# Attention output: probabilities normalised before they are turned, values as the stationary operand, heads summed in PSUM

## What is computed

```python
x = L0_attn_Z
xn = _layernorm(x); s = mamba(xn); g = _silu(moe0(xn))
x = x + s * g
xn = _layernorm(x, axis=-1)
s = _L1_attn_ref(xn, gamma, w_qkv, w_out)     # below
g = _silu(_L1_ffn_ref(xn, wg, we))            # top-2 of 128 experts
return x + s * g

# _L1_attn_ref
xn = x / jnp.maximum(l2, 1e-12) * scale_norm * gamma
q, k, v = per head of xn @ w_qkv.T            # q * 128 ** -0.5
sim = jnp.einsum('bihd,bjhd->bhij', q, k)
sim = jnp.where(causal_mask, neg, sim)
attn = jax.nn.softmax(sim, axis=-1)
out = jnp.einsum('bhij,bjhd->bihd', attn, v)
return jnp.einsum('bnf,cf->bnc', out.reshape(b, n, 1024), w_out)
```

## Time and profile before

| | us |
|---|---|
| median of 3 runs (1464.28 to 1469.84) | 1465.71 |
| span of the profiled execution | 1465.0 |
| PE busy over the span | 1277.5 (87%) |
| DVE busy over the span | 1227.2 (84%) |
| ACT busy over the span | 856.9 (58%) |
| attention stage, share of PE in 1275 to 1400 us | 125.00 of 125.00 |
| one iteration in that stretch | 7.20 |
| one iteration with expert products (about 1156 to 1271 us) | 8.19 |

### The profile page before, as it was taken

The page is one execution under the profiler, slowest core; times in us unless marked ns, Lnnn a source line. Parts: engine busy times, 40 slices in busy tenths (PEclk is TensorE's granted clock), DMA queues, the critical chain, the costliest instruction groups (busy, mean ns, idle before and its releaser), DMA issues. The chain is left out here.

```text
span 1465.0 us, 21638 instructions
## 1 busy us (share of the span) xinstructions
PE 1277.5 (87%) x7304; PEld 888.3 (61%) x7304; DVE 1227.2 (84%) x2515; ACT 856.9 (58%) x2077; POOL 661.9 (45%) x612
## 2 busy tenths in 40 slices
PE   6977888897887976899897895599999999999997
PEld 5533444453433444788887774467676777777776
DVE  6678999998999899999997778869988555568877
ACT  5357757665798885556654658554464444444462
POOL 0018555605489855664751775339600322147300
PEclk9997999999999877999999898699999999999999
DMA  6003545545244422454552520300020233113201
GB/s 230 1 21 87 147 128 147 141 122 153 82 126 126 123 87 68 126 155 135 146 146 72 190 53 13 119 7 1 2 59 1 60 89 107 41 38 49 25 16 43
DMA packets 75747, 127.50 MB, mean 87 GB/s; under 512 B 11486, under 2 KB 38334, under 8 KB 75030
## 3 DMA queue, kind: packets, MB, share of 16 engines
q1 hardware_dynamic: 56182, 75.24, 17.0%
q0 software_dynamic: 19456, 50.88, 13.2%
HBM read 85.71 MB, written 40.37 MB: 86 GB/s over the span
## 5 line engine op out<-in xcount | busy, mean ns | idle before, releaser
L672 DVE TENSOR_TENSOR_SCAN sc_st<-sc_dA,sc_st 128x1024 f32<-128x1024 f32 x128 | 287.3, 2284 | 0.0
L2164 DVE COPY at_pT<-at_p_t 128x512 f32<-128x512 f32 (+1 forms) x192 | 109.0, 598 | 107.8 <-PE at_p_t L2046 107.4
L1270 POOL DMA_INDIRECT g_state<-xn_scratch,moe_tab x96 | 119.6, 1246 | 174.3 <-POOLq L99 102.4
L2059 PEld LDWEIGHTS at_p_o<-at_V,at_pT 128*128 128x128 f32 x1280 | 154.4, 194 | 31.1 <-issue 30.8
L444 ACT ACTIVATE sc_dA<-sc_dt,g_state 128x511 f32<-128x511 f32 x256 | 168.9, 710 | 7.2 <-DVE sc_st L672 5.3
L650 DVE TENSOR_TENSOR sc_st<-sc_st,sc_p_bc 128x1024 f32<-128x1024 f32 x128 | 154.9, 1211 | 13.4 <-PE sc_p_bc L501 13.2
L640 DVE TENSOR_TENSOR sc_st<-sc_u,sc_p_bc 128x1024 f32<-128x1024 f32 x128 | 154.3, 1206 | 6.6 <-PE sc_p_y L532 6.3
L1310 POOL DMA_INDIRECT g_state<-r_scratch,moe_tab x96 | 121.5, 1266 | 83.6 <-PE e_bank L1409 56.7
L2059 PE MATMUL at_p_o<-at_V,at_pT 128*128 128x128 f32 x1280 | 155.0, 277 | 3.6 <-DVE g_state L2153 3.6
L2026 PE MATMUL at_p_s<-att_xaT,at_qT 128*128 128x512 f32 (+3 forms) x512 | 150.7, 437 | 0.0
L501 PE MATMUL sc_p_bc<-sc_bc,mamba_sel 96*128 96x512 bf16 x256 | 104.9, 411 | 50.5 <-DVE sc_st L640 48.6
(11 more groups left out here) (304 smaller groups left out, 2615.0 us busy)
## 6 DMA issues: line engine op xcount, KB each, us to landing
y_scratch<-g_state SPq DMA_DIRECT2D x24, 768.0 KB, 5.2
g_state<-W SPq DMA_DIRECT2D x48, 256.0 KB, 5.5
r_scratch<-g_state SPq DMA_DIRECT2D x16, 512.0 KB, 3.6
y_scratch<-g_state SPq DMA_DIRECT2D x24, 192.0 KB, 2.8
xn_scratch<-g_state SPq DMA_DIRECT2D x16, 256.0 KB, 4.9
g_state<-x SPq DMA_DIRECT2D x4, 512.0 KB, 7.5
g_state<-xn_scratch SPq DMA_DIRECT2D x8, 256.0 KB, 5.2
g_state<-x SPq DMA_DIRECT2D x1, 2048.0 KB, 12.7
```

The source lines that it names most:

```text
L672: nc.vector.tensor_tensor_scan(st[:, m % RS, :, :].rearrange("p a b -> p (a b)"), dA[:, m % 4, :, :].rearrange("p a b -> p (a b)"), st[:, ...
L1270: nc.gpsimd.indirect_dma_start(out=self.xg[:, e % 4, h, :], out_offset=None, in_=self.xn_rows, in_offset=bass.IndirectOffsetOnAxis(ap=r.ta ...
L2059: ins = nc.tensor.matmul(p_o[:, i, :], pT[:, n % 2, bank, c + (i - j) * P:c + (i - j + 1) * P], V[:, b % 2, j, h * D:(h + 1) * D], start=( ...
L2164: v.tensor_copy(pT[:, n % 2, part, 0:cols], p_t[:, PT_BANK[part], 0:cols]).then_inc(pT_ready, 1)
```

## The change

The reciprocal of the sums is taken before the turning (`invert`, on DVE, at the head of the iteration, for head n + 1), and ACT multiplies each row of probabilities by it in place (`normalise(n + 1)`, four ACTIVATEs with a pointer as scale, behind `copy_query`). `turn(n)` waits for that instead of for `exps`. In `weigh` the values stand still and the turned probabilities stream, 512, 384, 256 and 128 columns, so that `p_o` holds the transposed output, [128 features, 512 tokens]; the eight heads of a batch accumulate there, from `start` at the first head to `stop` at the last. `add_head` and its four instructions are gone. Once per batch ACT copies the sum to SBUF (`copy_out`, into a free part of `pT`), PE turns it back into `p_o` (`turn_out`, four transposes, after `turn` of the next batch's first head), and DVE copies it to `s_rows` (`take_rows`).

```diff
-        p_o = s.ps("p_o", [P, 4, D])
+        oT = pT[:, :, 2, 256:512]
+        p_o = s.ps("p_o", [P, L])
...
             def turn(n):
-                pe.wait_ge(exped, 3 * (n + 1))
+                pe.wait_ge(weighted, n + 1)
...
             def weigh(n):
                 b, h = divmod(n, NH)
                 pe.wait_ge(v_copied, NH * (b + 1))
-                if n:
-                    pe.wait_ge(out_used, n)
+                if h == 0 and b:
+                    pe.wait_ge(rows_taken, b)
                 pe.wait_ge(pT_ready, 3 * (n + 1))
-                for i in range(TB):
-                    for j in range(i + 1):
-                        bank, c = PT_AT[j]
-                        ins = nc.tensor.matmul(p_o[:, i, :], pT[:, n % 2, bank, c + (i - j) * P:c + (i - j + 1) * P],
-                                               V[:, b % 2, j, h * D:(h + 1) * D], start=(j == 0), stop=(j == i))
+                for j in range(TB):
+                    bank, c = PT_AT[j]
+                    ins = nc.tensor.matmul(p_o[:, j * P:L], V[:, b % 2, j, h * D:(h + 1) * D],
+                                           pT[:, n % 2, bank, c:c + L - j * P],
+                                           start=(h == 0 and j == 0), stop=(h == NH - 1 and j == TB - 1))
                 ins.then_inc(out_ready, 1)
+
+            def turn_out(b):
+                pe.wait_ge(oT_ready, b + 1)
+                for j in range(TB):
+                    ins = nc.tensor.transpose(p_o[:, j * P:(j + 1) * P], oT[:, j // 2, j % 2 * P:(j % 2 + 1) * P], w["ident"])
+                ins.then_inc(out_turned, 1)
...
             for n in range(NI):
                 turn(n)
+                if n and n % NH == 0:
+                    turn_out(n // NH - 1)
                 yield
...
+            turn_out(B - 1)
...
             def exps(n):
                 if n >= 4:
-                    act.wait_ge(out_used, n - 3)
+                    act.wait_ge(weighted, n - 3)
...
+            def normalise(n):
+                act.wait_ge(inverted, n + 1)
+                for i in (3, 2, 0, 1):
+                    bank, c = SIM_AT[i]
+                    row = pr[:, n % 3, bank, c:c + (i + 1) * P]
+                    ins = nc.scalar.activation(row, row, ACT.Copy, scale=sums[:, n % 4, i:i + 1])
+                ins.then_inc(weighted, 1)
+
+            def copy_out(b):
+                act.wait_ge(out_ready, NH * (b + 1))
+                if b:
+                    act.wait_ge(out_turned, b)
+                nc.scalar.activation(oT, p_o[:, :].rearrange("p (a b) -> p a b", a=2), ACT.Copy).then_inc(oT_ready, 1)
...
             exps(1)
+            normalise(0)
             for n in range(NI):
+                if n and n % NH == 0:
+                    copy_out(n // NH - 1)
                 if n + 3 < NI:
                     copy_query(n + 3)
+                if n + 1 < NI:
+                    normalise(n + 1)
                 yield
...
+            copy_out(B - 1)
...
-            def add_head(n):
-                b, h = divmod(n, NH)
-                link(v.reciprocal(sums[:, n % 4, :], sums[:, n % 4, :]))
-                dve.wait_ge(out_ready, n + 1)
-                for i in range(TB):
-                    o = s_rows[:, b * TB + i, :]
-                    if h == 0:
-                        ins = v.tensor_scalar(o, p_o[:, i, :], sums[:, n % 4, i:i + 1], None, ALU.mult)
-                    else:
-                        ins = v.scalar_tensor_tensor(out=o, in0=p_o[:, i, :], scalar=sums[:, n % 4, i:i + 1], in1=o,
-                                                     op0=ALU.mult, op1=ALU.add)
-                ins.then_inc(out_used, 1)
+            def invert(n):
+                dve.wait_ge(exped, 3 * (n + 1))
+                v.reciprocal(sums[:, n % 4, :], sums[:, n % 4, :]).then_inc(inverted, 1)
+
+            def take_rows(b):
+                dve.wait_ge(out_turned, b + 1)
+                v.tensor_copy(s_rows[:, b * TB:(b + 1) * TB, :].rearrange("p a d -> p (a d)"),
+                              p_o[:, :]).then_inc(rows_taken, 1)
 
             maxima(0)
             maxima(1)
+            invert(0)
             for n in range(NI):
                 yield
+                if n + 1 < NI:
+                    invert(n + 1)
+                if n > 1:
+                    dve.wait_ge(out_ready, n - 1)
                 for part in range(3):
                     dve.wait_ge(turned, 3 * n + part + 1)
...
-                if n > 1:
-                    dve.wait_ge(out_used, n - 1)
-                if n:
-                    add_head(n - 1)
+                if n and n % NH == 0:
+                    take_rows(n // NH - 1)
                 yield
                 if n + 2 < NI:
                     maxima(n + 2)
-            dve.wait_ge(out_used, NI - 1)
-            add_head(NI - 1)
+            take_rows(B - 1)
```

More of the change, by code:

```diff
@@ L1962, in attention_stage @@
         p_t = s.ps("p_t", [P, 2, 512])
-        p_o = s.ps("p_o", [P, 4, D])
+        oT = pT[:, :, 2, 256:512]
+        p_o = s.ps("p_o", [P, L])
         p_q = s.ps("p_q", [P, 512])
-        chain = s.sem("chain")
         q_product = s.sem("q_product")
@@ L1975, in attention_stage @@
         out_ready = s.sem("out_ready")
-        out_used = s.sem("out_used")
-        beside.s_rows_added = out_used
+        inverted = s.sem("inverted")
+        weighted = s.sem("weighted")
+        oT_ready = s.sem("oT_ready")
+        out_turned = s.sem("out_turned")
+        rows_taken = s.sem("rows_taken")
+        beside.s_rows_added = rows_taken
         block = ctx.enter_context(nc.Block())
@@ L2126, in scalar_steps @@
                     exps(n + 2)
+            copy_out(B - 1)
         def vector_steps(dve):
-            link = Chain(dve, chain)
             v = nc.vector
```

4 lines of the change are left out of this document (2 added, 2 removed).

## The result

| | before | after |
|---|---|---|
| median, us | 1466.28 (1464.28 to 1469.84, 4 runs) | 1484.47 (1482.4 to 1488.91, 4 runs) |
| ratio | | 1.0125, 95% interval 1.0103 to 1.0147 |
| span of the profiled execution | 1465.0 | 1480.6 |
| from the last of the first eight value products to the end | 495.7 | 514.2 |
| DVE busy over the span | 1227.2 | 1162.0 |

The change makes the kernel 18.2 us slower by the medians; 16.4 were forecast, and the range of 1470 to 1491 holds the result. The two profiled spans differ by only 15.6. In the profile of after, the code ahead of the attention's loop, which the change does not touch, took 2.84 us less: the eight first value products end at 964.53 + 1.88 = 966.41, and at 969.25 in the profile of before. In the nine profiles of this case that point lies between 964.9 and 973.5, so the 2.84 us lie within the spread of what stands ahead.

What follows compares the result with a forecast made beforehand. PE bounds the kernel, with a nearly equal chain through the exponentials beside it; stalls, longer iterations, turn_out and clock, less gains on DVE and at the end, sum to +16.4 us on 1465.7: 1482.1 us, range 1470 to 1491.

Steps and rivals of the forecast that it cites:

- The bound and the chain: Attention loop: exponentials, then reciprocal, hold copies and transposes; iterations 11 to 15 +0.75 each, expert iterations +0.25 each, +3.8 per group.
- the signs that were to show the forecast wrong: Copies starting before the exponentials end, expert iterations keeping 8.19 us, or no gap at the Silu.
- the late ones: 27 late iterations: chain level with now, 1294.51 against 1294.52, so 0 us, bounds -2 and +3; period still 7.2.
- The start and the clock: First transposes wait for the first normalising, +3.9 us; slower clock after the two new stalls, 1.2 us each, +2.4.
- The Silu: Iteration 56: Silu rows, table loads and normalising delay iteration 57's exponentials and so the copies; +5.4 us once.
- What DVE gains: DVE's freed time pays where it is late: one-hots, iterations 16 to 19, -2.1 us; iterations 7 to 10, -0.4.
- turn_out: Four transposes per batch on PE's path, 0.43 us, seven times: +3.0 us.
- the end: Last two `weigh` no longer wait for `add_head`, less clock loss, extra final steps: together -3.0 us, bounds -1 and -4.
- The first: Rival: the reciprocal does not hold the copies; +0.6 us, 1466.3; chance 0.12 of ending within 0.5% of 1465.7.
- The second: Rival: DVE was the hidden bound in the first 22 iterations; 1460.6 us; chance of over 0.5% faster 0.04.
- The third: Rival: wide products cost by the record, 1.3 us off `weigh`; about -5 us, 1477; chance 0.05.
- The fourth: Rival: ACT becomes the bound if normalising costs over 2.64 us; at 3.6 us, 1530; chance 0.03.

Runs made afterwards that it cites:

- the wait alone: Kernel before, plus one wait: ahead of its copies of iteration n's turned tile, DVE waits for the last exponential of iteration n+1; 1486.3 us, 1.0149 of the kernel before.
- the run that fills this room and 0.85 more: Changed kernel with eight small ACTIVATEs of 32 columns more behind each head's normalising on ACT; one run, 1522.21 us.
- the last kernel: Changed kernel: reciprocal behind copies, first head normalised on DVE, expert's step ahead of normalising, Silu and seventh batch's sum moved; 1459.98 us, 0.9964 of the kernel before.

## Why the prediction was right, and where it was not

**The bound and the chain.** Right. The chain value, value copy, exponentials, reciprocal, copy, transposes decides wherever it was said to: +0.78 an iteration in 11 to 15 (forecast 0.75), +0.19 with expert products (0.25). The changed kernel with the reciprocal moved back and the kernel before with the wait alone show it from both sides. None of the signs that were to show the forecast wrong came: the first transposes start at 971.08, which with the 2.84 us that were saved ahead is 973.92, and the copies start behind the exponentials.

**Its length was 0.1 too long.** I took 0.81 us from the start of a copy to the transposes; in the expert iterations it is 0.73 (1165.73 to 1166.46), and the reciprocal adds 0.13 from the last read to the copy, not 0.17. By this alone an expert iteration would cost 0.13 more and not 0.25; the two transposes that come behind the wait take 0.44 in place of 0.38, and with these 0.06 it is the 0.19 that was measured, 2.8 us and not 3.8 in all. In 11 to 15 the two steps measure 0.20 and 0.75, near the 0.98 counted, and with the same 0.06 the 0.75 became 0.78. The shorter chain is also why the late ones, which I saw as just level, have a little room and keep the 0.07 of `weigh`: -1.3 in place of 0. "The late period still 7.2" was wrong. Both are inside the bounds given.

**The start and the clock.** The wait was right to 0.02 us (973.9 - 970.03 = 3.87 counted, 3.89 measured). The clock behind it was not: 1.2 us counted, 2.6 shown by the run that kept PE busy. I took the 1.2 from a wait of 1.81 us; this wait is 4.67. But the 2.6 are of one profile: in two runs with the same wait, the reciprocal moved back and the expert's step moved ahead, the first `weigh` came 11.28 and 11.37 us behind the value products, in place of 12.25 in after and 9.70 with PE kept busy. There the clock cost 1.6 and 1.7.

**The Silu.** 9.51 - 4.27 = 5.24 us for the chain, 5.4 forecast, and 1.5 for the clock, 1.2 forecast. The one gap of over 3 us that should show it is two gaps, 1.91 and 2.78: the value copy, too, stands behind the Silu, and the `query` waits for it. The sum is the same because the exponentials end last.

**A step that was missing.** Iteration 22, +3.4. I listed what stands behind DVE's new wait, but for the normalising on ACT only the value copy and the exponentials. The copy of the first expert input stands there too, in this one iteration (later inputs are copied behind the value copy). The kernel that moves it ahead gets it all back. Its price, a wait of 1.8 us more and 1.5 us of lower clock, is more than the 2.1 us by which the sum fell short; the clock at the start (+1.4) and the shorter chain (-2.3) nearly cancel. That the sum came within 2.1 us is therefore in part luck: a place worth 3.4 us was left out, and the misses in the other terms, up and down, came to -1.3.

**What DVE gains, turn_out, the end.** -1.9, +3.0 and -3.3 against -2.1, +3.0 and -3.0; iterations 7 to 10 gain 0.9 in place of 0.4. In both groups the new wait hides part of what DVE gains: iteration 10 is 0.78 longer, like those behind it, and 17 is no shorter. With the reciprocal moved back the two groups gain 2.6 and 3.1 us over the kernel before.

**The rivals.** The first, that the reciprocal does not hold the copies, falls with the two runs on its place. The second, DVE as the hidden bound, is true where it was counted (iterations 7 to 10 and 16 to 19, 2.7 us in after, 5.6 with the reciprocal moved back) and hardly elsewhere. The third falls: `weigh` takes 2.16 with 8 records and took 2.23 with 20, so these fp32 products cost by their columns here. By the figures for a stream in the Trainium skill ("TensorE: Matmul & The Clock Gate", Back-to-back issue gap) `weigh` would have lost, as an estimate from that page, about half of its time; the trace does not agree. The fourth: the normalising takes 1.9 us on ACT, as estimated (1.8), and fits into the idle time with 0.84 to spare; the run that fills this room and 0.85 more pays 35 us. The Trainium skill ("ScalarE: Activation LUTs", Rules for kernel authors) sends multiplications to VectorE. The traces agree on the price (1.27 us on VectorE in the last kernel against 1.90 on ScalarE in after, for the same four), but in the steady iteration the dearer engine costs nothing.

## What to carry to other kernels

A wait put ahead of work on an engine that takes its instructions in order is paid where its releaser is later than that work was; ask it of every kind of iteration, since here the late ones had under 0.1 us of room and the ones with other work on ACT had none. For each step that is moved to another engine, list all that stands behind it there, the work that comes only once included: the one iteration with the first expert's input cost more than the fifteen that follow. When the places are known, most of such a loss can be mended one by one, and the gains of the change then show: 0.36% faster than before in place of 1.25% slower.

## What the runs showed of the hardware

- PE's clock fell to its lower level (0.50, 1.2 GHz) behind waits of 4.67, 2.49 and 2.32 us, in which PE did nothing; with products in the longest of them it stayed at 1.00. Behind a wait of 1.81 us it fell in one of two places in the kernel before and in both with the wait alone (3.99 and 4.07 us for a `weigh` that takes 2.47); behind 2.00 us at the Silu of the last kernel it stayed at 1.00. So the length of a wait near 2 us does not tell, and the cost of a wait varies: iteration 56 takes 13.79 us in after, and 15.11 in two kernels whose code there is the same; behind the same 4.67 us the first `weigh` came after 12.25, 11.28 and 11.37 us.
- PE worked at the lower level for 3 to 4 us behind the wait of 2.49, and for some 5, or again 3 to 4, behind that of 4.67; at the Silu in after the level lasted 7 us, the second wait included. What decides this was not tried.
